# Wave's constant rows: four 32-column products side by side and one closing sum

## The reference

```python
for l in range(L):                                   # L = 2
    e = h @ ent_w[l] + ent_b[l]                      # 256 -> 1024
    ent = e @ ent_pw[l] + ent_pb[l]                  # 1024 -> 256
    h = _layer_norm(h + ent, ln3_g[l], ln3_b[l])
    t = jnp.einsum('bsd,pdf->pbsf', h, path_w[l]) + path_b[l][:, None, None, :]
    ...
```

## Time and profile before

| | us |
|---|---|
| median of three runs | 1016.67 (1016.58 to 1016.80) |
| the profiled execution | 1016.39 |
| its span, first to last instruction | 1014.2 |
| PE busy in the span | 973.5 |
| DVE busy | 758.5 |
| ACT busy | 609.6 |
| POOL busy | 361.0 |

### The profile page before, as it was taken

How to read it: one execution, slowest core, us unless ns; L and a number is a source line. 1 busy time by engine, 2 the same in 40 slices (tenths; PEclk the granted TensorE clock), 3 DMA queues, 4 the chain that set the end, 5 groups by cost and what they waited for, 6 DMA issues and landing times.

```text
span 1014.2 us, 18311 instructions
## 1 busy us (share of the span) xinstructions
PE 973.5 (96%) x6483; PEld 806.4 (80%) x6483; DVE 758.5 (75%) x2089; ACT 609.6 (60%) x1177; POOL 361.0 (36%) x646
## 2 busy tenths in 40 slices
PE   8899999999899898999999999999999999999997
PEld 7566555656558798787899999999999999999897
DVE  6666777776847778967767687877778787687874
ACT  6455767656558774645745566665566665566650
POOL 4435356373231374443832222223222232222420
PEclk9899999999979999999999999999999999999999
DMA  7000011012020001022111220221112022121111
GB/s 258 24 1 22 23 33 43 19 36 63 22 89 1 4 2 42 1 104 63 36 49 24 74 67 26 63 64 27 52 46 65 22 64 63 32 63 32 48 46 54
DMA packets 55043, 47.42 MB, mean 47 GB/s; under 512 B 7108, under 2 KB 52392, under 8 KB 54952
## 3 DMA queue, kind: packets, MB, share of 16 engines
q1 hardware_dynamic: 52632, 43.75, 14.2%
q10 hardware_dynamic: 2320, 2.49, 0.8%
HBM read 31.40 MB, written 4.20 MB: 35 GB/s over the span
## 4 chain that ended last, share of the span: by engine, by line
PE 54%; DVE 5%; POOL 2%; issue 1%; ACT 1%; DVEq 0%; POOLq 0%; ACTq 0%
PE ps L1991 24%; PE ps L2008 24%; PE ps L1889 2%; DVE ln_stats L2409 1%; PE ps L2021 1%; PE ps L1940 1%; POOL hs L1786 1%; DVE xT_l L2543 0%; POOL x_b L1786 0%; PE ps L1903 0%; DVE amp L2445 0%; PE ps L1918 0%; DVE G_l L2549 0%; PE ps L1931 0%; PE ps L1840 0%
## 5 line engine op out<-in xcount | busy, mean ns | idle before, releaser
L2245 ACT ACTIVATE G<-ps,bias_col 128x512 f32<-128x512 f32 x192 | 135.8, 707 | 156.6 <-PE ps L1991 148.1
L2008 PE MATMUL ps<-w_l,G_h 128*128 128x256 f32 x736 | 203.8, 277 | 0.0
L2008 PE MATMUL ps<-w_h,G_l 128*128 128x256 f32 x736 | 203.8, 277 | 0.0
L2008 PE MATMUL ps<-w_h,G_h 128*128 128x256 f32 x736 | 203.7, 277 | 0.0
L2549 DVE TENSOR_TENSOR G_l<-G,G_h 128x512 fp32r<-128x512 f32 x192 | 166.2, 866 | 48.2 <-ACT G_h L2246 48.2
L1816 POOL TENSOR_TENSOR x_a<-xn,mlp_g 128x1024 f32<-128x1024 f32 x20 | 56.0, 2800 | 326.7 <-DVE xn L2575 326.7
L721 ACT ACTIVATE probs<-ps 128x512 f32<-128x512 f32 (+3 forms) x256 | 98.5, 441 | 95.8 <-PE ps L857 95.1
L1991 PE MATMUL ps<-xT_h,w_h 128*128 128x512 f32 x384 | 150.3, 391 | 0.6 <-DVE xT_l L2543 0.4
L1991 PE MATMUL ps<-xT_h,w_l 128*128 128x512 f32 x384 | 149.7, 390 | 0.0
L1991 PE MATMUL ps<-xT_l,w_h 128*128 128x512 f32 x384 | 149.5, 389 | 0.0
L2008 PEld LDWEIGHTS ps<-w_h,G_h 128*128 128x128 f32 x736 | 138.4, 188 | 0.9
(11 more groups left out here) (330 smaller groups left out, 2103.4 us busy)
## 6 DMA issues: line engine op xcount, KB each, us to landing
w_raw<-L_ffn_W_T SPq DMA_DIRECT2D x12, 1024.0 KB, 5.4
landed<-squares SPq DMA_DIRECT2D x320, 32.0 KB, 1.9
hs<-L_attn_hidden_states SPq DMA_DIRECT2D x8, 512.0 KB, 3.9
x_kept<-hs SPq DMA_DIRECT2D x4, 512.0 KB, 3.3
w_raw<-x_kept SPq DMA_DIRECT2D x2, 1024.0 KB, 5.5
out<-xn SPq DMA_DIRECT2D x3, 512.0 KB, 2.8
w_raw<-L_ffn_ent_w_T SPq DMA_DIRECT2D x1, 1024.0 KB, 9.3
w_raw<-L_ffn_ent_pw SPq DMA_DIRECT2D x1, 1024.0 KB, 11.5
```

The lines of the kernel that those rows point to most:

```text
L2008: mm = pe.matmul(ps[:, 4 + t // 2, (t % 2) * D:(t % 2 + 1) * D], x[b % 2][f][:, t * P:(t + 1) * P], w2_chunk(w, f), start=(k == 0), stop=( ...
L2245: act.activation(G32[n % 4], bank, ACT.Gelu, bias=bias)
```

## The change

The four slots stay, with other contents. The first of each pair is now the whole sum over 1024 in eight products (`constant`): product m streams chunk m and writes only the 32 partitions of quarter m % 4, so chunks 0 and 4 add up in the first quarter, 1 and 5 in the second, and so on. DVE copies the 128 x 256 result, four different partial sums, into the row of `stage_c`. The second slot (`total`) multiplies that with weights that are all 1/32: each output partition gets the sum over 128 partitions divided by 32, which is the sum of the four partial sums. DVE adds `ent_pb` to it. The 1/32 stands in a third column of `turns`, filled by one more memset. SP's and POOL's waits that named the second half of a sum now name the grouped sum.

```diff
-            (3, 0, "entangle", (0, 1, 1)), (3, 3, "constant", (0, 0)), (5, 2, "constant", (0, 1)))
+            (3, 0, "entangle", (0, 1, 1)), (3, 3, "constant", 0), (5, 2, "total", 0))
...
-           (2, 1, "entangle", (1, 1, 1)), (3, 1, "constant", (1, 0)), (4, 0, "constant", (1, 1)),
+           (2, 1, "entangle", (1, 1, 1)), (3, 1, "constant", 1), (4, 0, "total", 1),
...
+GROUP_ROWS = 32
...
-                    sp.wait_ge(s["p_work"], WORK.number(0, "first", ("constant", (0, 1))))
+                    sp.wait_ge(s["p_work"], WORK.number(0, "first", ("constant", 0)))
...
+            elif kind == "total":
+                pe.wait_ge(g.wave["v_turns"], 3)
+                pe.wait_ge(s["work_read"], WORK.number(i, when, ("constant", arg)) + 1)
+                mm = pe.matmul(work[:, 0:D], g.turns[:, 2:3].broadcast_to([P, P]), g.stage_c[:, 2 * arg + 1, :],
+                               start=True, stop=True)
+            elif kind == "constant":
...
+                pe.wait_ge(s["v_bias"], 1)
+                for m in range(MC0):
+                    rows = slice(m % 4 * GROUP_ROWS, (m % 4 + 1) * GROUP_ROWS)
+                    col = 4 + arg * MC0 + m
+                    mm = pe.matmul(work[rows, 0:D], g.bias_col[:, col:col + 1].broadcast_to([P, GROUP_ROWS]),
+                                   raw_pw[:, m, :], start=(m < 4), stop=(m >= MC0 - 4))
...
+        v.memset(g.turns[:, 2:3], 1.0 / GROUP_ROWS).then_inc(g.wave["v_turns"], 1)
...
+                chain.settle()
+                v.tensor_copy(g.stage_c[:, 2 * arg + 1, :], work[:, 0:D]).then_inc(s["work_read"], 1)
+            elif kind == "total":
+                v.tensor_tensor(g.stage_c[:, 2 * arg + 1, :], work[:, 0:D], ent_pb[:, arg, :], ALU.add
+                                ).then_inc(s["work_read"], 1)
...
-        sp.wait_ge(first["p_work"], WORK.number(B - 1, "last", ("constant", (1, 1))))
+        sp.wait_ge(first["p_work"], WORK.number(B - 1, "last", ("constant", 1)))
...
-        pool.wait_ge(first["p_work"], WORK.number(B - 1, "last", ("constant", (1, 1))))
+        pool.wait_ge(first["p_work"], WORK.number(B - 1, "last", ("constant", 1)))
```

More of the change, by code:

```diff
@@ L273, in build @@
         g.last_b = put(nc, "last_b", g.small, 20 * D - 80 - D, [D])
-        g.turns = sb(top, nc, "turns", [P, 2])
+        g.turns = sb(top, nc, "turns", [P, 3])
         attention0(nc, A, g, top)
@@ L930, in use_work @@
                 mm = pe.transpose(work[:, 0:BIAS_COLS], bias_rows[:, :], ident[0:BIAS_COLS, 0:BIAS_COLS])
-            elif kind in ("entangle", "constant"):
+            elif kind == "total":
[4 more added lines that the diff above has]
+            elif kind == "constant":
+                if arg:
+                    pe.wait_ge(s["ent_in"], 32 * MC0)
+                else:
+                    pe.wait_ge(g.pre["w1_in"], 16)
+                pe.wait_ge(s["v_bias"], 1)
[4 more added lines that the diff above has]
+                                   raw_pw[:, m, :], start=(m < 4), stop=(m >= MC0 - 4))
+            elif kind == "entangle":
                 l, part = arg[0], arg[-1]
@@ L937, in use_work @@
                     pe.wait_ge(g.pre["w2_in"], 16)
-                if kind == "constant":
-                    pe.wait_ge(s["v_bias"], 1)
                 for n in range(MC_HALF):
                     m = part * MC_HALF + n
[L942 to L947, removed]
+                    mm = pe.matmul(work[:, 0:D], ent_t[:, m, arg[1] * P:(arg[1] + 1) * P], raw_pw[:, m, :],
+                                   start=(n == 0), stop=(n == MC_HALF - 1))
             elif kind == "offset":
@@ L1214, in take_work @@
                 if arg == 2:
-                    v.wait_ge(s["work_read"], WORK.number(i, when, ("constant", (1, 1))) + 1)
+                    v.wait_ge(s["work_read"], WORK.number(i, when, ("total", 1)) + 1)
                 v.tensor_tensor(g.stage_c[:, at, :], g.stage_c[:, at, :], work[:, 0:D], ALU.add
@@ L1319, in entry @@
                     next(work_ahead)
-                if kind in ("project", "out", "bias", "entangle", "constant", "offset"):
+                if kind in ("project", "out", "bias", "entangle", "constant", "total", "offset"):
                     take_work(i, when, kind, arg)
@@ L1462, in first_sine @@
     if b == 0:
-        act.wait_ge(g.wave["v_turns"], 2)
+        act.wait_ge(g.wave["v_turns"], 3)
     act.activation(g.half[:, b, :, :], g.tanh[:, b, :, :], ACT.Sin, bias=g.turns[:, 0:1],
```

## The result

| | before | changed |
|---|---|---|
| median, us | 1016.42 (1014.87 to 1016.80, 6 runs) | 1007.41 (1004.30 to 1011.76, 6 runs) |
| the profiled execution | 1016.39 | 1004.30 |
| its span | 1014.2 | 1002.3 |
| its mean granted clock | 0.985 | 0.996 |

The ratio is 0.9926 [0.9905, 0.9947]: 0.74% less time where 0.44% was forecast. It is not the ratio of the two medians, which lie 9.0 us (0.89%) apart; in the experiments, too, the two differ by up to 0.2%. The median lies 2.6 us under the lower end of the range. The single runs now spread over 7.5 us, and their mean granted clocks go with them: 0.996 at 1004.3, 0.986 at 1011.8.

The account below looks back on a forecast made before the run. TensorE's order was taken to set the pace at the four places: 7.69 - 2 x 0.99 - 2 x 0.63 = 4.45 us off 1016.39, plus 0.28 for the median, gives 1012.2 us, range 1010.0 to 1014.2.

Parts of the forecast that it names:

- The removed and added products: TensorE, four constant-row sums: 7.69 us removed, grouped sums 2 x 0.99 and totals 2 x 0.63 added.
- the four places: Slots (3,3), (5,2) of entry 0 and (3,1), (4,0) of entry 3: together 4.45 us less.
- Four quarters side by side: Grouped sum: 32-column products in four partition quarters overlap, so eight hold TensorE for 0.99 us.
- the quarters take turns: Rival, 3%: the grouped sum's products do not overlap and take 3.64 us; kernel at 1017.5 us.
- The waits: At the four places the gains of 0.93, 1.30, 0.93, 1.29 us fit into VectorE's idle times.
- VectorE takes over: Rival, 9%: half of each gain at the four places goes into waits for maxima; 1014.4 us.
- The memset: At the start, ahead of the memset releasing TensorE: one more may cost up to 0.06 us, counted as nothing.
- Wave and MLP keep their length: After the attention: the wave stages should keep their lengths.
- the clock moves, fewer or shorter: Rival, 12% of the clock's 24%: fewer or shorter attention stretches at clock 0.50; one fewer gives 1010.9 us.
- the slots with the clock at 0.50 differ from those of before: Sign that the forecast is wrong: lower-clock slots in the profile after are not those of before.
- the price of a short stretch: Entry 1, about 147.8 to 151.1 us: one short stretch at clock 0.50 costs 1.34 us.
- the most that the long one could give: Entry 3, 284.3 to 297.9 us at clock 0.50: at most 6.4 us, a third of that expected at most.

Follow-up runs that it names:

- e5: The changed kernel once more, unaltered, on another chip; 1008.44 us, ratio 0.9936 against the kernel before.
- e1: Only layer 0's row (entry 0) made the new way, layer 1's as in the kernel before; 1008.70 us, ratio 0.9944.
- e4: The kernel before with five more unread products in slot (3,3) of entry 0, 2.15 us later; 1018.49 us, ratio 1.0024.
- e12: e1 with one unread product of 0.43 us ahead of the grouped sum in (3,3); 1014.21 us, ratio 1.0007 against the kernel before.
- e15: e1 with four unread products of 0.43 us each ahead of the grouped sum in (3,3); 1013.63 us, ratio 0.9993 against the kernel before.
- The fills: Unread products put where TensorE waits, in the opening and entries 1 to 3, in the changed kernel or the kernel before; medians 1002.70 to 1008.95 us.
- e11: The changed kernel with only four unread products at the end of the opening; 1006.20 us, ratio 0.9915 against the kernel before.
- the later fills: Unread products in TensorE's waits in entries 1 to 3; alone 1004.48 us in the changed kernel, 1008.95 us in the kernel before.
- e8: The changed kernel with unread products in TensorE's waits in entries 1 to 3 and four at the opening's end; 1002.70 us, ratio 0.9877.
- e10: e8 again, on another round of runs; 1002.78 us, ratio 0.9880 against the kernel before.

## Why the prediction was right and wrong

- **The removed and added products: right.** Grouped sum 0.98 (0.99 forecast), total 0.63 (0.63), the four places 4.52 (4.45). At one clock, by the line through all runs, the changed kernel lies 4.6 us under the kernel before in the first comparison and 5.0 in e5. In one of its first six runs the mean clock was 0.986, near before's 0.985: it took 1011.76 us, 0.4 from the forecast.
- **Four quarters side by side: right**, so "the quarters take turns" is out. The Trainium skill (TensorE: Matmul & The Clock Gate, section on the measured speedup of packing) would have given an estimated 1.22 us for the grouped sum; the trace, with 0.98, does not agree with it.
- **The waits: right.** VectorE's idle time ahead of the four readings went from 1.05, 1.92, 1.17, 1.50 to none, 0.63, 0.28 and 0.20 (0.1, 0.6, 0.2 and 0.2 forecast); the tightest gain fitted. TensorE's waits for the maxima up to 300 us are 6.9 us after [7.2 in rows 2], so "VectorE takes over" is out.

```profile
PE ps L847 <- DVE top_score L1148: 6.9, 12, 1.0
```

- **The memset: right at nothing.** TensorE's first instruction stood at 1.81 us and now stands at 1.84. Of the 0.29 us that the opening gained, the last section shows how its clock differs from run to run.
- **Wave and MLP keep their length: right**, 716.1 us in both.
- **The failed step: the stretches at the lower clock were taken to stay as they are.** The sum holds no term for the clock, so it stands at nothing. The rival "the clock moves, fewer or shorter" happened, and the slots with the clock at 0.50 differ from those of before, which the prediction had named as a sign of being wrong. The text had its mechanism, the price of a short stretch (1.34 us forecast, against a slot of another entry; 1.51 and 1.52 measured, against the same slots) and the most that the long one could give (6.4), but gave it 12%, let it count for one stretch at a time, and cut the long one by a third at most. Measured: both short stretches gone and 4.0 us off the long one in the profile. Over all runs the mean clock went from 0.987 (79 runs of before) to 0.991 and 0.988 (e5), which is 27 us at the lower level cut to 17 and 24; at 0.29 us each that is 2.7 and 0.9 us on top of the direct part. The rest of the 9.0 us between the medians of the first comparison, some 1.8, would fit the draw of the runs, which is argued and not shown: its six runs of before were all at 1014.9 or above, with a median of 1016.42 against 1015.3 to 1015.5 in every later comparison, while of the 55 runs of before beside e1 to e4 and e12 to e15, 14 stood at 1011.2 to 1012.1 with a clock of 0.991 or 0.992.
- **Why that was missed.** The rival was argued from how dense the work is: "what moves up behind them is as dense as the rest". How dense a place is does not decide alone. The stretch ahead of the fall in entry 1 is in the changed kernel too, with the same waits and the same busy time, and no fall follows:

```profile
141.70:145.00 3.30, 2.43 (x21) 1.55 (x22) 2.90 (x10) 1.18 (x4) 2.75 (x6) 1.00 0.00 0
145.10:148.40 3.30, 3.30 (x32) 1.84 (x29) 1.72 (x8) 1.84 (x5) 0.88 (x4) 1.00 0.02 5
```

  That TensorE was at work when the clock fell was also the prediction's ground against idling as the cause. The fills show that its short waits do bear on the falls: with the 0.94 us ahead of 31.40 filled, the first stretch is gone.

  A kernel with four stretches at the lower clock in a part that the change shifts has a second source of scatter, here up to 9 us wide from run to run (e11) and 5.5 in the medians between e1 and e12. The three runs of before, within 0.2 us, hid it, and the range had no room for it.

What stays open: why a thin spot brings a fall in one kernel and not in another, and which of the later filled waits matter.

## What to carry to other kernels

Price an edit by rows of the same shape, and write that part of the forecast down apart from the clock: at one clock, by the line, it held to 0.3 us in the ten kernels without the later fills (to 0.6 in e5, the changed kernel once more); those with the fills lie another 0.5 to 0.9 us lower. Where the trace shows stretches at the lower clock in the part that moves, ask what each of them would give back if it went and widen the range by all of them together, to both sides; then judge variants at equal mean clock, and don't credit the edit with the rest. If such stretches follow waits of TensorE in busy code, fill the waits with products that nobody reads: it took no more here than a free bank to write into, gave about as much as the change itself, and in the changed kernel, with all of them in (e8, e10), made the times repeat to 1 us.

## What the runs showed of the hardware

- The clock changes are not tied to the program. In the opening, ahead of any edited product, the same eight transposes take 1.82 us in the profiled execution of before, 1.50 in that of the changed kernel and 1.04 in that of e5, which is the same kernel again. The profile gives no clock for these first microseconds. The products of one line around the transposes tell it: before, ten of them start at 0.44 us a product ((6.25 - 1.81) / 10), and four behind the transposes at 0.25 ((8.82 - 7.82) / 4), so the rate rises in between, at another moment in each execution. Before, after, and e5:

```profile
1.81 4.64 PE L1022 MATMUL ps<-neg_max 128*128 128x512 f32 x10 [1.81 <-DVE neg_max L1119]
6.25 1.82 PE L1030 MATMUL ps<-ident,hs 128*128 128x128 f32 x8
7.82 1.17 PE L1022 MATMUL ps<-neg_max 128*128 128x512 f32 x4
8.82 0.37 PE L1043 MATMUL ps<-wqkv_h,x_h 128*128 128x384 f32 x1
```

```profile
1.84 4.64 PE L1033 MATMUL ps<-neg_max 128*128 128x512 f32 x10 [1.84 <-DVE neg_max L1131]
6.29 1.50 PE L1041 MATMUL ps<-ident,hs 128*128 128x128 f32 x8
```

```profile
1.84 4.48 PE L1033 MATMUL ps<-neg_max 128*128 128x512 f32 x10 [1.84 <-DVE neg_max L1131]
6.16 1.04 PE L1041 MATMUL ps<-ident,hs 128*128 128x128 f32 x8
```

  The Trainium skill (TensorE: Matmul & The Clock Gate, section on what is actually happening) says that the chip's watch on TensorE's activity runs freely, so that one kernel sees the change at different moments from run to run. The traces agree, and add that the falls inside a busy attention differ too between two executions of one kernel: e5's profile has a stretch from 262 to 276 us where the first one of the changed kernel has none. The six times of that kernel, 1004.3 to 1011.8 us, go with their mean clocks.
- A microsecond at the lower level cost 0.29 us here on the average of the 202 runs, not half of one. It depends on the place: the short stretches cost 1.51 and 1.52 us for some 3.3 each, the long one 4.01 for 13.6. In the long one VectorE, ScalarE and GpSimd are busy for 4.89, 7.15 and 6.81 us of 13.6, in a short one for 0.61, 1.38 and 0.41 of 3.3; that they set more of the pace in the long one would fit, but no run tests it.
- Eight float32 products of 32 columns in two rounds over four quarters take what a value pass of the same streamed columns takes, 0.98 against 0.99 us: the border between the rounds costs nothing that shows.
